# Delta rule: one inverse for the four token tiles of a call, and a call's walk beside the next call's inverse

## What is computed

```python
def step(state, inp):
    q_t, k_t, v_t, a_t, b_t = inp
    retained = jnp.einsum('bhvk,bhk->bhv', state, k_t)
    rk = retained[..., None] * k_t[:, :, None, :]
    vk = v_t[..., None] * k_t[:, :, None, :]
    state = a4 * (state - b4 * rk) + b4 * vk
    o_t = jnp.einsum('bhvk,bhk->bhv', state, q_t)
    return (state, o_t)
```

## Time and profile before

| | |
|---|---|
| median of 3 runs | 3619.95 us (3609.34 to 3629.92) |
| span of the profiled execution | 3635.6 us |
| its time, against the median | 15.7 us (0.4%) above |
| PE (matmul) busy | 3157.9 us, 87% |
| DVE busy | 2261.0 us, 62% |
| ACT busy | 1429.1 us, 39% |
| POOL busy | 932.4 us, 26% |

### The profile page before, as it was taken

The page is one execution under the profiler, slowest core; times in us unless marked ns, Lnnn a source line. Parts: engine busy times, 40 slices in busy tenths (PEclk is TensorE's granted clock), DMA queues, the critical chain, the costliest instruction groups (busy, mean ns, idle before and its releaser), DMA issues.

```text
span 3635.6 us, 86922 instructions
## 1 busy us (share of the span) xinstructions
PE 3157.9 (87%) x35006; PEld 2198.3 (60%) x35006; DVE 2261.0 (62%) x5812; ACT 1429.1 (39%) x3328; POOL 932.4 (26%) x851
## 2 busy tenths in 40 slices
PE   5689988888898888898868989876889999999989
PEld 5367666666676666766657867665445545544544
DVE  6566778666778666678446645635546556556555
ACT  1544444444444444344136622124333433433331
POOL 0112231412222412222405526432212212221110
PEclk7898988899998899899679989988879999999999
DMA  6111211302111301211347754285111111111000
GB/s 239 41 37 45 66 47 30 130 28 63 57 49 48 118 26 49 60 49 38 101 152 187 195 164 137 93 257 178 40 41 42 35 42 47 36 41 43 5 18 18
DMA packets 224091, 280.89 MB, mean 77 GB/s; under 512 B 35072, under 2 KB 172464, under 8 KB 223312
## 3 DMA queue, kind: packets, MB, share of 16 engines
q1 hardware_dynamic: 184448, 216.93, 18.4%
q0 software_dynamic: 34896, 54.20, 6.7%
q10 hardware_dynamic: 4352, 4.20, 0.3%
HBM read 184.64 MB, written 90.62 MB: 76 GB/s over the span
## 4 chain that ended last, share of the span: by engine, by line
PE 66%; DVE 18%; ACT 5%; issue 4%; DMA 3%; POOL 1%; DVEq 0%; ACTq 0%; SPq 0%; POOLq 0%
PE banks L3054 6%; PE banks L570 5%; DVE s_d_kq L663 3%; PE banks L1940 3%; PE banks L2589 3%; PE banks L809 2%; PE banks L1282 2%; PE banks L2575 2%; PE banks L1949 2%; PE banks L2601 2%; PE banks L796 2%; PE banks L970 2%; PE banks L968 2%; PE banks L2845 2%; PE banks L2755 2%
## 5 line engine op out<-in xcount | busy, mean ns | idle before, releaser
L570 PE MATMUL banks<-s_d_xT,s_w_qkvg 128*128 128x512 f32 x640 | 345.3, 667 | 14.8 <-DVE s_d_kq L663 9.6
L663 DVE SCALAR_TENSOR_TENSOR s_d_kq<-banks,s_conv_w,s_d_kq 128x511 f32<-128x511 f32 (+2 forms) x384 | 286.0, 745 | 53.2 <-ACT s_d_kq L615 43.4
L2717 ACT ACTIVATE s_g_pT<-banks 128x1536 f32<-128x1536 f32 (+1 forms) x96 | 152.8, 1592 | 365.7 <-PE banks L2591 365.7
L3054 PE MATMUL banks<-s_m_we,s_m_tT 128*128 128x512 f32 x512 | 234.5, 603 | 6.0 <-DVE s_m_x L3117 6.0
L615 ACT ACTIVATE s_d_kq<-banks,s_conv_w 128x512 f32<-128x512 f32 x128 | 87.9, 687 | 282.1 <-PE banks L570 281.5
L641 ACT ACTIVATE s_d_square<-banks 128x128 bf16<-128x128 f32 x512 | 134.6, 278 | 158.6 <-PE banks L599 158.4
L570 PEld LDWEIGHTS banks<-s_d_xT,s_w_qkvg 128*128 128x128 f32 x640 | 125.6, 210 | 117.5 <-issue 90.0
L1940 PE MATMUL banks<-s_q_xsT,s_q_w 128*128 x1008 | 162.1, 285 | 37.0 <-issue 27.9
L2674 DVE TENSOR_REDUCE s_g_off<-banks 128x4 f32<-128x512 f32 (+2 forms) x96 | 117.2, 1220 | 123.0 <-PE banks L2575 120.9
L1940 PEld LDWEIGHTS banks<-s_q_xsT,s_q_w 128*128 128x128 f32 x1008 | 156.2, 199 | 60.2 <-issue 47.3
L796 PEld LDWEIGHTS banks<-s_d_Xc,s_d_Mc 32*32 32x32 f32 x8192 | 92.2, 115 | 129.5 <-DVE s_d_Xc L909 54.8
(11 more groups left out here) (415 smaller groups left out, 7714.7 us busy)
## 6 DMA issues: line engine op xcount, KB each, us to landing
s_q_w<-w12p SPq DMA_DIRECT2D x128, 257.0 KB, 6.3
s_q_xs<-xs SPq DMA_DIRECT2D x32, 516.0 KB, 5.6
s_d_E<-sums SPq DMA_DIRECT2D x64, 256.0 KB, 3.4
s_r_xT<-xfT SPq DMA_DIRECT2D x12, 1024.0 KB, 7.0
tree<-s_r_bias SPq DMA_DIRECT2D x96, 128.0 KB
s_r_work<-xf SPq DMA_DIRECT2D x24, 512.0 KB, 4.5
og<-s_d_o SPq DMA_DIRECT2D x16, 512.0 KB, 3.0
sorted<-s_q_acc SPq DMA_DIRECT2D x32, 256.0 KB, 2.1
```

Of the source, the lines that this page charges most:

```text
L570: ins = e.matmul(bk[6 + j % 2][:], w[:, par, c, self.COL[what] + h * P:self.COL[what] + (h + 1) * P], xT[:, c, :], start=(c == 0), stop=(c ...
L663: e.scalar_tensor_tensor(d[:, a:], bk[6 + j % 2][:, 0:SEQ - a], cw[:, par, k0 + 3 - a:k0 + 4 - a], d[:, a:], ALU.mult, ALU.add).then_inc(s ...
L2717: e.activation(self.pT[c][:], psum[:, 0:4, 0:self.COLUMNS[c]], ACT.Exp).then_inc(self.exped, 1)
L3054: ins = e.matmul(self.product_bank(b, k, q)[:], self.tT[:, c, t * P:(t + 1) * P], self.we[:, c, (2 * half + q) * 512:(2 * half + q + 1) * ...
```

## The change

The four tiles of a call are inverted together: M, the compact blocks (`Xc`, `XT`, `TB`) and `Pf` hold all 16 of them, one level product is 64 products of 32x32 and one eviction 512 columns. There is one list of 34 steps per call (setup 10, six levels of 4). The whole walk of a call, four tiles, runs beside the next call's setup and first two levels. Behind each level product stands one unread product, whatever the level, and none at level 6. X is no longer put together whole and turned by TensorE: level 5 makes the turned block as well (operands exchanged, L801, L802), the diagonal blocks of `Pf` are copied from `XT` by ScalarE (L880), and only a 64-row part of X (`X6`) is kept for level 6. The decays are loaded into `Dm` itself, two sets of four tiles, and overwritten in place with the masked q k. R, U, T1 and S are parts of one tile `walked`, which also takes the squares of o, so `o2` goes; `upper` and `ones` lie in M, and `Mc` is `TB`.

```diff
     def walk(self, e, decays, project, invert, state, beside, first=None):
...
-            ahead = project(e, n + 1) if n + 1 < self.CALLS else iter(())
-            main, here = invert(e, n, 0), state(e, n, 0)
-            side_by_side((next(main) for _ in range(6)), (last, 0.5), (ahead, 0.67))
-            side_by_side(main, (last, 0.64), (ahead, 0.8), (beside, 0.62))
+            ahead, main = project(e, n + 1) if n + 1 < self.CALLS else iter(()), invert(e, n)
+            side_by_side((next(main) for _ in range(self.SETUP)), (last, 1.2), (ahead, 0.9), (beside, 0.5))
+            side_by_side((next(main) for _ in range(2 * self.LEVEL)), (last, 2.3), (ahead, 1.6), (beside, 1.0))
             finish(last)
-            main = invert(e, n, 1)
-            side_by_side((next(main) for _ in range(6)), (ahead, 1.34))
-            side_by_side(main, (here, 0.5), (ahead, 0.8), (beside, 0.62))
-            finish(here, ahead)
-            last = state(e, n, 1)
+            side_by_side(main, (ahead, 1.8), (beside, 1.0))
+            finish(ahead)
+            last = state(e, n)
...
-    UNREAD = (0, 0, 0, 1, 2, 2)
+    UNREAD = (0, 1, 1, 1, 1, 1)
+    SETUP, LEVEL = 10, 4
...
+                if l < 5:
+                    for b in range(4):
+                        r = slice(32 * b, 32 * b + 32)
+                        ins = e.matmul(bk[2][r, c], XT[r, a, :], TB[r, a, :], start=True, stop=True)
+                else:
+                    e.matmul(bk[2][0:32, c], TB[32:64, a, :], XT[32:64, a, :], start=True, stop=True)
+                    e.matmul(bk[2][64:96, c], TB[96:P, a, :], XT[96:P, a, :], start=True, stop=True)
+                    ins = e.matmul(bk[2][32:64, c], XT[32:64, a, :], TB[32:64, a, :], start=True, stop=True)
...
+    def invert_scalar(self, e, n):
...
+        for half in range(2):
+            e.wait_ge(self.T_made, 7 * n + 6 + half)
+            e.activation(self.T6[:, 8 * half:8 * half + 8], bk[half][64:P].rearrange("p (a n) -> p a n", n=64), ACT.Copy).then_inc(self.B_made, 1)
+        self.diagonal_scalar(e, 0)
+        yield
+        if n + 1 < self.CALLS:
+            self.decays_scalar(e, n + 1)
+        yield
+        e.wait_ge(self.Z_made, 7 * n + 7)
+        e.activation(Pf[0:64, 8:16, 64:P], bk[3][0:64].rearrange("p (a n) -> p a n", n=64), ACT.Copy).then_inc(self.P_half, 1)
+        yield
+
+    def diagonal_scalar(self, e, pair):
+        for b in (2 * pair, 2 * pair + 1):
+            ins = e.activation(self.block(self.Pf, b, b), self.XT[32 * b:32 * b + 32], ACT.Copy)
+        ins.then_inc(self.P_diagonal, 1)
...
+    def invert_gpsimd(self, e, n):
...
+            if step == 23 and n + 1 < self.CALLS:
+                self.decays_gpsimd(e, n + 1)
...
+    def state_gpsimd(self, e, n):
...
+        if n:
+            e.wait_ge(self.o_normed, 4 * n - 3)
+        e.memset(self.S, 0.0).then_inc(self.S_zero, 1)
+        for _ in range(24):
+            yield
+        e.wait_ge(self.stepped, 28 * (n + 1))
+        e.tensor_tensor(self.walked[:], self.o[:], self.o[:], ALU.mult).then_inc(self.o_squared, 1)
```

475 lines of the change are left out of this document (207 added, 268 removed).

## The result

The changed kernel takes **3824.68 us** (median of 4 runs, 3808.76 to 3834.69) against 3614.72 for the kernel before on the same chip: 1.0551 times, 95% interval 1.0503 to 1.0599. The prediction was 3561 us, in a range of 3490 to 3680: wrong in sign, and outside the range.

The account below looks back on a forecast made before the run. DVE, with PE close behind, was taken to bound a call's first half, PE and its waits the second. Pieces of 14.1 + 61.5 + 26 made 101.6 us against 105.8, fourteen times: -59, so 3576 us profiled, 3561 predicted, range 3490 to 3680.

Parts of the forecast that it names:

- Piece 1: Call boundary: first walk product waits for the zeroed state behind ACT's tail and POOL; 11.1 us stall plus 3, 14.1 us.
- Piece 2: From the boundary to the projections' last tap: 56 us of DVE work at 91% busy, 61.5 us; bounds 56 to 68.
- The 91%: DVE's assumed busy share up to the last tap, taken from old first halves at 82, 84 and 89%.
- Piece 3: From the last tap to the call's last product: 21.6 us, 26 at a clock of 0.77; bounds 21 to 31.
- ACT without a break: After the last tap: about 6.7 us to the first squares, then ACT continuously busy; 20.9 us, 21.6 with small gaps.
- PE's 102 us: PE work said to go, 6.4 us a call: 192 unread products (67.4 us) and X's transposes (41.9), less 7.3 added.
- a clock under 0.85: Sign in the profile after: a PE clock under 0.85 would say that the unread products were too few.
- The rivals: Alternatives to the forecast: PE-bound with more gain, chance 0.14; no change, 0.17; slower by the boundary stall, 0.23.
- the slower one: Boundary chain ACT to POOL to PE's in-order queue stalls 20 us: 110.5 us a call, +66, 3686 us; chance 0.23.

Follow-up runs that it names:

- quiet run at 0.98: Changed kernel, routing's steps done after the calls, state zeroed early, 32 unread products a call instead of 10: 99.1 us a steady call.
- quiet unedited one at 0.74: Changed kernel with only the routing's steps taken out of the sixteen calls and done afterwards: 102.1 us a steady call.
- 46 products: Changed kernel, routing's steps done after the calls, state zeroed early, 46 unread products a call instead of 10: 98.9 us a steady call.
- quiet kernels: Kernels with the routing's steps done after the calls: changed kernel with state zeroed early, 99.1 us a steady call; kernel before, 93.4.
- early-zeroed quiet run: Changed kernel, routing's steps done after the calls, memset of the state moved ahead of v's scaling: 99.1 us a steady call.
- quiet kernel before: Kernel before with the routing's steps taken out of the calls and done afterwards: 93.4 us a steady call, against 105.8 with routing.

## Why the prediction was wrong, step by step

**Piece 1, the boundary: right in mechanism, sized too high, and its loss too.** Predicted 11.1 us of stall and 3 of products. Measured from the call's first setup product to the walk's first 7.3 us on average over the steady calls (1.5 to 13.7), of which the wait is 77.8 / 14 = 5.6 (the other 11 of the 88.8 us stand in the last call), and then some 3.5, mostly at half clock: 10.8 us. Without the wait the time falls by 2.3%.

**Piece 2, to the last tap: one of the two steps that failed.** It was to take 61.5 us because DVE would be busy for 91% of it. The work was right: I counted 56 us of DVE, and the first stretches have 54.9 on average. The 91% was not. With 82.1 us on average from the call's start to the last tap, the piece took 71 us instead of 61.5, outside the 68 given as its end: DVE was busy 70% of the first stretch, and even if all of that lay in piece 2, with up to 3.5 us more for the last taps, it would be 82%. I took the share from first halves in which half as much of the walk stood. Each tile of walk is a chain PE, DVE, PE, DVE through two in-order queues; put twice as densely beside projections it makes each engine wait for the other. That reading rests on waits and is not shown: no run changed the walk's rate. DVE's waits for the walk's first product went from 23.7 us (L1004 before) to 170.3 (L998), but more than half of that is piece 1 again, since they fall to 76.4 with the memset early, and some of the rest stands in the last call, where the walk runs alone.

**Piece 3, to the last product: the other step, and the larger miss, 36.5 us instead of 26**, outside its end of 31. "ACT without a break" was wrong in its last words: ScalarE is busy for 21.4 us of the 36.47 shown above, as counted, and idle for the rest. The 26 were for a clock of 0.77, 21.6 before that. The clock was right (0.77 on average in the second stretches), the sum was not, even without the routing: in the quiet run at 0.98 piece 3 is 27.5 us (99.1 less 71.7 to the last tap), in the quiet unedited one at 0.74 it is 31.0. So 5 to 6 us are waits in the piece itself, where squares, decayed k and transposes go round between ACT, DVE and PE: DVE waits 99.0 us for squares in the stage. The routing adds the other 5.5 or so (the two are of different kinds of chip); the three calls with the scatters are 16 us longer each than the others, 3.4 us a call. Those I had costed at nothing, having looked at the stall ahead of GpSimd's gathers and never at DVE's own two copies.

The three pieces make 10.8 + 71.3 + 36.5 = 118.6. The first call came 10 us shorter and the last 22 longer than before (138.5 against 116.5, to the end of the last walk product); predicted were 20 each way, cancelling.

**PE's 102 us.** The work went and the busy time stayed: 1505 us in the stage against 1481. I had written that a clock under 0.85 would mean too few unread products. It is 0.79 to 0.81, and that reading was too simple. In the rows PE's idle time a call doubled and the clock fell from 0.90 to 0.81. The Trainium skill (TensorE: Matmul & The Clock Gate, "Why this matters for your kernels") warns of idle gaps between bursts of products; the rows agree in direction. The gaps here are short ones, though: in the lone walk of before, which the prediction called in agreement with that page, the waits before its half-clock products are 1.44 and 0.85 us in the earlier trace rows. And filling the gaps raised the clock to 0.94 (46 products) and left the call at 98.9 us, so here the low clock is more a sign of a call bound by its chain than the bound itself.

**The rivals.** The one with the right sign was the slower one, at 0.23: a boundary stall, priced at 3686 us, and the time was 139 us above that. The stall explains 2.3% of the 5.5, the scatters about 0.8% (a comparison across chips). What is left is 2.3%, 78 us by the medians and 46 between the profiled executions (spans of 3681.4 and 3635.6). There the steady call is 109.3 us against 105.8, 48 us over fourteen calls, and the last call 15 longer, the first 9 shorter. The quiet kernels differ by more, 99.1 - 93.4 = 5.7 us a call (the run with 32 products, also 99.1, is of one kind of chip with the 93.4); that 14 x 5.7 = 80 stands so near the 78 is chance. That difference needs no routing, no memset and no shortage of unread products. At an equal clock of 0.94 the account closes: the quiet call with 46 products takes 98.9 us against 93.4, since it holds 12.5 us of unread products where before has 7.1, has 3.3 us less of other PE work, and idles 3.4 us more. That this idle time is the crossing of walk and setup and the tail of ScalarE is what the waits point to (L971, L978, L784). It was not taken apart further, so the cause of this part stays open.

## What to carry to other kernels

When a change packs a serial chain more densely beside parallel work, don't carry the busy share of the old mix over to the new one: count how often the chain crosses between in-order queues, and try the chain's rate by itself. Work off the path gives nothing until the chain at the boundary is shorter, and a wait that is removed shows the next link of the same chain. A side stream that is paced by steps must be looked at again when the steps get shorter, down to its smallest instruction, since a 0.17 us copy that waits for a DMA holds everything behind it.

## What the runs showed of the hardware

The granted clock and the time can part company. For one instruction stream calls of 92.7 and 104.6 us went with clocks of 0.92 and 0.78, yet raising the mean clock from 0.80 to 0.94 with idle products moved the mean call by 0.6 us. No wait of PE in the early-zeroed quiet run was longer than 3.0 us, and its clock was 0.83 all the same, where the quiet kernel before with waits up to 2.8 us had 0.94. And a ratio belongs to where it was measured: the same two kernels gave 1.055 where the kernel before takes 3615 us and 1.038 where it takes 3721.
